# A gated cross-attention and channel-mix block: x normalised in its transposed layout by GpSimd, side work of the attention loop reordered

## The reference

```
xn  = layernorm(x)                        # over the 512 features, eps 1e-5
Q   = xn @ Wq.T + bq;  K = ctx @ Wk.T + bk;  V = ctx @ Wv.T + bv
S   = Q K^T / sqrt(32), masked;  A = softmax(S)       # 16 heads of 32
x1  = x + tanh(g1) * ((A V) @ Wo.T + bo)
z   = layernorm(x1);  zp = z shifted by one position (0 in front)
r   = sigmoid((mu_r z + (1-mu_r) zp) @ Wr.T)
k   = relu((mu_k z + (1-mu_k) zp) @ Wk2.T) ** 2
out = x1 + tanh(g2) * r * (k @ Wv2.T)
```

## Time and profile before

| what | before |
|---|---|
| median of 3 runs | 1231.34 us |
| the profiled execution | 1232.68 us |
| its span | 1230.8 us |
| PE (TensorE matmul) busy | 1167.7 us, 95% |
| VectorE (DVE) busy | 942.5 us, 77% |
| ScalarE (ACT) busy | 745.2 us, 61% |
| GpSimd (POOL) busy | 237.4 us, 19% |
| DMA moved | 110.33 MB, mean 90 GB/s |

### The profile page before, as it was taken

The page is one execution under the profiler, slowest core; times in us unless marked ns, Lnnn a source line. Parts: engine busy times, 40 slices in busy tenths (PEclk is TensorE's granted clock), DMA queues, the critical chain, the costliest instruction groups (busy, mean ns, idle before and its releaser), DMA issues.

```text
span 1230.8 us, 22178 instructions
## 1 busy us (share of the span) xinstructions
PE 1167.7 (95%) x7424; PEld 921.5 (75%) x7424; DVE 942.5 (77%) x2011; ACT 745.2 (61%) x1619; POOL 237.4 (19%) x427
## 2 busy tenths in 40 slices
PE   3999999999999999999999999977999999999997
PEld 2777776777777777777677777754888888888886
DVE  5778788788878887878878887879677677777763
ACT  4578778678768877877867876764432333233232
POOL 2030030030021003003003000024423433332431
PEclk9999999999999999999999999987999999999999
DMA  6433342253243333344225322452111311311200
GB/s 218 120 94 83 101 122 66 63 157 81 71 129 89 81 102 100 82 104 118 67 60 159 78 74 65 123 168 76 59 52 60 95 52 52 104 52 52 97 25 35
DMA packets 72703, 110.33 MB, mean 90 GB/s; under 512 B 14864, under 2 KB 23696, under 8 KB 72592
## 3 DMA queue, kind: packets, MB, share of 16 engines
q1 hardware_dynamic: 72592, 108.92, 31.1%
HBM read 41.76 MB, written 16.78 MB: 48 GB/s over the span
## 4 chain that ended last, share of the span: by engine, by line
PE 76%; DVE 9%; issue 6%; ACT 4%; DMA 4%; SPq 1%; POOL 0%; POOLq 0%; ACTq 0%; DVEq 0%
PE bank L445 24%; PE bank L509 14%; PE bank L476 12%; PE bank L521 10%; PE bank L502 7%; PE bank L485 6%; DMA x_rows<-x 3%; DVE neg_s L857 3%; ACT probs L681 2%; PE bank L491 2%; PE bank L575 1%; DVE pT L863 1%; DVE xh L973 1%; DMA pT<-wkT 1%; DVE ctx_sb L848 1%
## 5 line engine op out<-in xcount | busy, mean ns | idle before, releaser
L681 ACT ACTIVATE probs<-neg_s,negmax 128x512 f32<-128x512 f32 x512 | 367.9, 720 | 40.5 <-DVE negmax L857 39.4
L857 DVE CUSTOM_DVE_ANT_0 neg_s<-bank,mask_big 128x512 f32<-128x512 f32 x512 | 344.7, 683 | 19.2 <-PE bank L502 16.9
L509 PE MATMUL bank<-ident,probs 128*128 128x128 f32 x2048 | 314.8, 276 | 17.3 <-ACT probs L681 16.8
L509 PEld LDWEIGHTS bank<-ident,probs 128*128 128x128 f32 x2048 | 240.4, 141 | 75.6 <-ACT probs L681 40.7
L863 DVE COPY pT<-bank 128x512 f32<-128x512 f32 x256 | 176.5, 690 | 120.8 <-PE bank L509 119.7
L502 PE MATMUL bank<-k_stack,q_stack 96*128 96x512 f32 x512 | 243.3, 475 | 6.0 <-DVE negmax L857 5.9
L688 ACT COPY pT<-bank 128x512 f32<-128x512 f32 x256 | 149.4, 584 | 98.3 <-PE bank L509 92.5
L1068 POOL TENSOR_SCALAR var_eps<-mv 128x2 f32<-128x2 f32 (+1 forms) x24 | 18.5, 770 | 639.9 <-DVE mv L822 578.3
L521 PE MATMUL bank<-pT,v_sb 128*32 128x512 f32 x1024 | 118.5, 603 | 0.8 <-issue 0.5
L779 ACT ACTIVATE relu<-bank 128x512 f32<-128x512 f32 x32 | 19.2, 598 | 149.0 <-PE bank L445 149.0
L502 PEld LDWEIGHTS bank<-k_stack,q_stack 96*128 96x128 f32 x512 | 97.3, 190 | 11.2 <-DVE negmax L857 8.5
(11 more groups left out here) (110 smaller groups left out, 2125.1 us busy)
## 6 DMA issues: line engine op xcount, KB each, us to landing
k_stack<-k_hi SPq DMA_DIRECT2D x256, 64.0 KB, 2.0
q_stack<-q_hi SPq DMA_DIRECT2D x256, 64.0 KB, 2.0
x_rows<-x SPq DMA_DIRECT2D x8, 1024.0 KB, 6.6
cT_raw<-ctxT SPq DMA_DIRECT2D x8, 1024.0 KB, 5.8
k_stack<-k_lo SPq DMA_DIRECT2D x128, 64.0 KB, 2.0
q_stack<-q_lo SPq DMA_DIRECT2D x128, 64.0 KB, 2.0
ctx_dram<-ctx_sb SPq DMA_DIRECT2D x32, 256.0 KB, 2.1
c_raw<-ctx_dram SPq DMA_DIRECT2D x16, 512.0 KB, 5.1
```

The source lines that it names most:

```text
L509: mm = nc.tensor.transpose(pt_bank[i % 2][:, a * P:(a + 1) * P], probs[:, i % P_RING, a * P:(a + 1) * P], ident[:])
L681: nc.scalar.activation(probs[:, i % P_RING, :], neg_s[:, i % SM_RING, :], ACT.Exp, bias=negmax[:, k:k + 1], scale=-1.0, accum_out=den[:, g ...
L857: nc.vector.tensor_tensor_reduce(neg_s[:, i % SM_RING, :], s_bank[i % S_BANKS][:], mask_big[:, q, :], 1.0, 3e38, ALU.add, ALU.min, negmax[ ...
```

## The change

x of the next batch is no longer turned by TensorE. The host also passes x turned (`xT_d`). Rows of x are loaded in four 256 KB pieces only for the statistics; mean and reciprocal root are written to DRAM (`mr_dram`) and read back into all partitions. GpSimd subtracts and multiplies in the turned layout, ScalarE rounds to `xT_hi`, GpSimd makes `xT_lo`, and GpSimd makes the low parts of ctx too. `x_rows` now holds two row buffers (or mean and root) and two buffers of turned x. The T and C items leave the loop; every group now has one K, one V and one Q. V 1 moves from the prologue into group 0. The statistics of batch b+2 begin in group 3 of batch b.

```diff
 PE_SIDE = [
-    parts("K", 1, 0, 1, 3, 4) | parts("V", 2, 6, 7, 8, 9, 10, 11) | parts("Q", 2, 12, 13, 14, 16),
-    parts("K", 2, 0, 1, 3, 4) | parts("V", 3, 6, 7, 8, 9, 10, 11) | parts("Q", 3, 12, 13, 14, 16),
-    {step: [("T", n, 0, 1)] for n, step in enumerate((0, 1, 3, 4))} | parts("K", 3, 5, 6, 7)
-    | parts("Q", 4, 9, 10, 12, 13, 14, 16),
-    parts("K", 4, 0, 1, 2) | parts("V", 0, 3, 4, 5, 6) | parts("V", 1, 7, 8, 9, 10)
-    | parts("Q", 5, 11, 12, 13, 14, 15, 16),
+    parts("K", 1, 0, 1, 3, 4) | parts("V", 1, 5, 6, 7, 8, 9, 10) | parts("Q", 2, 12, 13, 14, 16),
+    parts("K", 2, 0, 1, 3, 4) | parts("Q", 3, 6, 7, 8, 9) | parts("V", 2, 10, 11, 12, 13, 14, 15),
+    parts("K", 3, 0, 1, 3, 4) | parts("V", 3, 5, 6, 7, 8, 9, 10) | parts("Q", 4, 12, 13, 14, 16),
+    parts("K", 4, 0, 1, 3, 4) | parts("V", 0, 6, 7, 8, 9, 10, 11) | parts("Q", 5, 12, 13, 14, 16),
 ]
-PE_SIDE[2][TILES] += [("C", n, 0, 1) for n in range(CH)]
-STATS_STEPS = (8, 10, 12, 14)
+def stats_at(nb):
+    return ((0, 0, 8), (0, 0, 10), (0, 1, 1), (0, 1, 3)) if nb == 1 else (
+        (nb - 2, 3, 8), (nb - 2, 3, 10), (nb - 1, 0, 3), (nb - 1, 0, 5))
+def x_hi_at(nb):
+    return ((0, 2, 0), (0, 2, 1), (0, 2, 7), (0, 2, 8)) if nb == 1 else (
+        (nb - 1, 1, 10), (nb - 1, 1, 11), (nb - 1, 2, 2), (nb - 1, 2, 3))
+def c_hi_at(nb):
+    return tuple((nb - 1, 2, i) for i in (11, 12, 13, 14))
 # SP
+            def load_rows(b, t):
...
+                if t >= 2:
+                    sp.wait_ge(bn_done, b * TT + t - 1)
+                sp.dma_start(x_rows[:, t % 2, :],
+                             x[bass.ds(b * S, S), :].rearrange("(p t) c -> t p c", t=TT)[t]).then_inc(rows_ld[t % 2], 16)
+            def load_xT(b, a):
+                if b > 1 or a >= 2:
+                    sp.wait_ge(x_lo, (b - 1) * CH + (a - 1 if a >= 2 else 0))
...
+            def broadcast_mean_rstd(b):
+                sp.wait_ge(mr_copy, b)
+                sp.wait_ge(pool_chain, (b + 1) * CHAIN)
+                sp.dma_start(mr_dram[b].rearrange("(k p t) -> p k t", k=2, p=P), mean_rstd[:]).then_inc(mr_st, 16)
+                sp.wait_ge(mr_st, b * 16)
+                sp.dma_start(x_rows[:, 0:2, :].rearrange("p k t -> p (k t)"),
+                             mr_dram[b:b + 1, :].to_broadcast([P, 2 * S])).then_inc(mr_ld, 16)
             def batch(b):
                 for c in range(GROUPS):
-                    if c == 0 and not is_last(b):
-                        sp.wait_ge(side_done, done(b * SIDE_PER_BATCH + len(PROLOGUE) - 1))
-                        load_x(b + 1)
+                    if b + c == 0:
+                        load_rows(1, 0)
+                        load_rows(1, 1)
+                        load_xT(1, 0)
+                        load_xT(1, 1)
                     if c:
                         store_context(b, c - 1)
...
                         stack_group(b, c + 1)
                     if c == 0 and not is_last(b):
                         load_ctx(b + 1)
+                    if b == 0 and c == 0:
+                        load_rows(1, 2)
+                        load_rows(1, 3)
+                    if c == (1 if b == 0 else 0) and not is_last(b):
+                        broadcast_mean_rstd(b + 1)
+                    if c == 1 and not is_last(b):
+                        load_xT(b + 1, 2)
+                        load_xT(b + 1, 3)
+                    if c == GROUPS - 1 and b + 2 < B:
+                        for t in range(TT):
+                            load_rows(b + 2, t)
+                        load_xT(b + 2, 0)
+                        load_xT(b + 2, 1)
 # VectorE
             def row_stats(b, t):
-                if t == 0:
-                    dve.wait_ge(x_ld, b * 16 + 16)
-                    dve.wait_ge(mv_done, b * TT)
+                if b:
+                    dve.wait_ge(rows_ld[t % 2], ((b - 1) * 2 + t // 2 + 1) * 16)
...
 # GpSimd
+            def centre(b, a):
+                pool.wait_ge(xT_ld[a % 2], ((b - 1) * 2 + a // 2 + 1) * 16)
+                pool.wait_ge(mr_ld, b * 16)
+                nc.gpsimd.tensor_tensor(x_rows[:, 2 + a % 2, :], x_rows[:, 2 + a % 2, :], x_rows[:, 0, :],
+                                        ALU.subtract).then_inc(x_mid, 1)
+            # scale_rows: x_mid -> multiply by row 1 -> x_hat;  x_rest: x_hi -> xT_lo -> x_lo;  c_rest: ct_hi -> cT_lo
```

More of the change, by code:

```diff
@@ L411, in batch @@
                 store_context(b, GROUPS - 1)
-            for b in range(B - 1):
+            for b in range(B):
                 batch(b)
-            batch(B - 1)
             for s in range(2):
@@ L631, in step2 @@
                     o_proj(b + 1, h)
-            for b in range(B - 1):
+            for b in range(B):
                 step2(b, 0)
                 step2(b, 1)
-            step2(B - 1, 0)
-            step2(B - 1, 1)
         @block.scalar
@@ L712, in tile_step @@
                     probs_out(b, c, i)
[L714 to L719, removed]
             def batch(b):
                 for c in range(GROUPS):
-                    for i in range(EARLY if c == 0 else 0, TILES):
+                    for i in range(TILES):
                         tile_step(b, c, i)
+                        if b and (c, i) == (0, HI_STEP):
+                            side(b - 1, "R", GROUPS - 1)
+                        if not is_last(b) and (b, c, i) in x_hi_at(b + 1):
+                            x_rounded(b + 1, x_hi_at(b + 1).index((b, c, i)))
+                        if not is_last(b) and (b, c, i) in c_hi_at(b + 1):
+                            c_rounded(b + 1, c_hi_at(b + 1).index((b, c, i)))
                         if is_last(b) and (c, i) in SPLIT_W2:
@@ L749, in context_hi @@
                 nc.scalar.copy(c_hi[:], c_raw[:, h]).then_inc(c2_hi, 1)
-            early_steps(0)
-            for b in range(B - 1):
+            for b in range(B):
                 batch(b)
-            batch(B - 1)
             def xT_out(b, h):
@@ new lines, in c_rest @@
+            def c_rest(b, a):
+                pool.wait_ge(ct_hi, (b - 1) * CH + a + 1)
+                nc.gpsimd.tensor_tensor(act_lo[1][:, a, :], cT_raw[:, a, :], act_hi[1][:, a, :],
+                                        ALU.subtract).then_inc(ct_lo, 1)
+            rstd_of(0)
+            for b in range(1, B):
+                rstd_of(b)
+                for pair in ((0, 1), (2, 3)):
+                    for a in pair:
+                        centre(b, a)
+                    for a in pair:
+                        scale_rows(b, a)
+                    for a in pair:
+                        x_rest(b, a)
+                for a in range(CH):
+                    c_rest(b, a)
```

135 lines of the change are left out of this document (77 added, 58 removed).

## The result

The change is slower: 1335.66 us, the median of 4 runs (1332.17 to 1338.73), against 1231.63 for the kernel before beside it; the ratio is 1.084, interval 1.0815 to 1.0873. That is 104 us more where 81 were forecast, 1335.66 against 1312.7 us. One execution of a later run, the one with both edits, took 1653.50 us at a mean granted clock of 0.655, and is left out of that run's ratio. The profiled execution took 1338.73 us, 106.05 more than the one before.

What follows compares the result with a forecast made beforehand. The prediction took TensorE to set the pace. Its terms, -25.6 + 78.6 + 25.6 + 2.8 = +81.4 us, on the profiled 1232.68 gave 1314.1, and a median 1.34 lower: 1312.7 us, range 1278 to 1336.

Steps and rivals of the forecast that it cites:

- What becomes less: T transposes leave TensorE, waits in groups 0 and 2 shrink: 25.6 us less in seven batches (bounds 18 and 31).
- The wait in group 3: VectorE's statistics wait for row loads behind SP's stacking: 10.5 us plus 2.6 for the clock, six batches, +78.6 us.
- The wait in group 1: ScalarE's high part of Q 3 waits for SP's stacking: 3.2 us in all eight batches, +25.6 us.
- I leave the clock at full: In group 1 the granted clock stays at 1.00 despite the wait, so no clock cost is added.
- rival 4: More waits: reciprocals copy waits for GpSimd, 17 us, 1330; or clock falls in group 1, 21 us, 1333; together 0.17.
- The ends: Prologue nothing, last batch 0.3 us, batch 0's late second half of turned x 2.5 us; sum 2.8 us.
- Rival 1: Both waits vanish because SP's stacking issues take far less time: 1208.5 us, chance 0.03.
- Rivals 2 and 3: Only the wait in group 1 is real, 1234 us, chance 0.04; only that in group 3, 1287 us, chance 0.12.

Runs made afterwards that it cites:

- the one with both edits: The change with group 3's first two row loads issued ahead of the stacking and Q of group 3 written later in group 1: 1233.32 us.
- The last run: The change with its waits taken out, plus V 2 in steps 5 to 10 and Q 3 in steps 12, 13, 14, 16 of group 1: 1206.44 us.
- the first two runs: Each against the change: two row loads issued ahead of group 3's stacking, 1251.60 us; Q of group 3 written later in group 1, 1315.13 us.

## Why the prediction was right, and where it was off

**What becomes less: right in sum, with one part wrong.** I forecast 25.6 us for seven batches without new waits. The last run shows 100.0 - 96.2 = 3.8 us a batch, 26 to 27 us. Group 3 without waits is 23.6, as forecast within 0.2; group 0 kept 1.0 us instead of 1.3. Group 2 kept 1.6 instead of 0.7: "since ScalarE still does eight tile-sized roundings for x and c in a batch, six of them in this group" was a right reason with too small a size. With the x roundings in steps 6 and 7 instead of 2 and 3 group 2 fell from 25.15 to 24.95, and with the last two roundings of ctx beside the context matmuls as well to 24.5.

**The wait in group 3: right in mechanism, too small.** Forecast 10.5 us, measured 11.7 on average. The row load landed 3.3 to 3.9 us after its issue, 3.5 on average, not 2.3: as much as the whole difference. The issue itself came at 19.5 on average where I took 19.3; only in batch 2, where the first six stacking issues took 5.10 us and not the 3.7 of the other five batches, did it come at 20.3. The clock cost 2.2, not 2.6. Per group 14.2 against 13.1, in six groups 6.6 us too little. The run with the loads ahead of the stacking shows the cause directly.

**The wait in group 1: right in mechanism and size, but two terms are missing beside it, and they are the largest error.** The term "3.2 us in all eight batches: +25.6" stands against a group that rose by 43.9. The wait is not what was too small: TensorE's eight waits sum to 25.3. The first missing term is the clock. "I leave the clock at full" failed in six of the eight groups (0.89 to 0.94 in them), which was the second half of rival 4. Without its wait a group 1 takes 24.8 us in the two batches at full clock and 25.7 to 27.8 in the six others: an estimate of 8.9 us for the clock, where rival 4 had 21. The second is the group itself: those 24.8 us are 1.2 more than 23.54, 9.8 in eight groups, which I had nowhere in the sum. It goes with the places of the side items, since with Q 3 and the x roundings at the group's end the group takes 23.55; which of the moved items costs it while Q 3 stands in steps 6 to 9 was not tried. SP's coming late, for which I took 0.2 us and at most one more, is real in batch 2 alone (5.1 us into the group instead of 3.1). There it and a slower landing of the last DMA, 2.8 us after its issue and not 2.0, made the longest wait.

**The ends.** The prologue gained 0.6 us: it does wait for the stacking. Batch 0 was forecast at +2.5 and lost only 0.9 in its group 2, but because its group 1 was late as well; with that wait gone it loses 6 to 8. The reason was another than the forecast's, too. ScalarE waited there for the first half of turned x, since mean and root came late; before the second half it waited less than 0.1 us. That the term did the sum little harm is luck.

**The rivals.** Rival 1 did not come about: the pace of SP's issues stayed at 0.6 us. Rivals 2 and 3 fall with the first two runs. Of rival 4 the clock came, and the copy of the reciprocals took longer beside GpSimd's work, without a cost. The timelines of VectorE and GpSimd near the end of group 1 of batch 2 show it:

```profile
327.56 1.57 DVE L928 COPY rden_rep<-rden 128x512 f32<-128x512 f32 x1
```

```profile
327.56 2.71 POOL L1137 TENSOR_TENSOR x_rows<-x_rows 128x512 f32<-128x512 f32 x2
```

The copy took 1.57 us instead of the 0.43 of the earlier trace rows, with GpSimd's two operations beside it. This agrees with the rule of the Trainium skill, "SBUF — State Buffer", section "SBUF: two separate sides", by which one of the two holds a shared pair of ports for its whole instruction and the other waits. It is hidden under the context matmuls, as the forecast had it. TensorE's timeline has them from 327.89 to 331.53, and turns the copied values at 331.47, with no idle time in front, 2.3 us after the copy's end:

```profile
327.89 3.64 PE L574 MATMUL bank<-pT,v_sb 128*32 128x512 f32 x32 [0.49 <-issue]
331.47 0.66 PE L544 MATMUL bank<-ident,rden_rep 128*128 128x128 f32 x4
```

That the lock is what holds the copy was not tried by itself.

## What to carry to other kernels

A load that is moved to an earlier use must be moved in its queue too: read, in the issuing engine's order, what stands between the last signal and the load, and multiply by the pace of an issue. Freeing work from the engine that sets the pace gives its full worth only when no consumer in that loop waits for the queue; here 25 us of gain were hidden under some 130 us of waits and slow clock that a few moved lines took away. One batch is not the kernel: batch 2 had the longest wait of both kinds, and SP's late start was to be found in it alone. And take out one wait at a time, but don't expect the savings to stop where they appear: one wait can cover another.

## What I had not expected of the hardware

A wait of TensorE of 2.4 to 4.8 us was enough, in six of eight groups 1, for the clock to fall to 0.50 for some time: in group 1 of batch 2, with 0.46 us of matmuls in the first 5 us, it was 0.50 over the next six, at work, and back at 0.99 after it.

```profile
314.00:319.00 5.00, 0.46 (x4) 0.26 (x3) 0.97 (x2) 1.21 (x3) 0.60 (x1) 0.92 0.39 94
319.00:325.00 6.00, 5.77 (x24) 5.48 (x25) 2.86 (x8) 4.26 (x12) 2.56 (x2) 0.50 0.51 148
325.00:332.00 7.00, 6.51 (x56) 3.71 (x55) 4.95 (x10) 2.98 (x8) 5.20 (x4) 0.99 0.02 7
```

The group had a clock of 1.00 in batches 5 and 6, where TensorE waited 3.0 and 2.3 us, and fell to 0.94 in batch 4, where it waited 2.4; so the length of the wait alone does not say which it will be. Even shorter ones can do it: in the run with Q of group 3 written later, every group 1 of batches 1 to 6 has waits of TensorE of 1.06 and 0.85 us near its end, and in one of these six, batch 1, the clock fell.

Work that ends 3.6 us before the wait does saves little: the clock fell behind 8.9 us of matmuls as behind none, if for a shorter time, and the stretch behind it took 12.5 to 12.7 us in five of six groups, where full speed gives 11.2 and the plain change 13.0 to 13.8. A store of 4 KB takes 5.2 to 5.8 us when it is issued behind a load of 1 MB in the same queue (six batches of the change), and 1.7 to 3.0 ahead of it (six batches of the run with the round trip first).
